# Sums by an adding DMA from GpSimd's queue in place of two GpSimd passes, and a second one-sided part written by ScalarE

## The reference

```python
def attn(x):                      # 16 heads of 16 features, L = 512
    U = min(L, int(5 * math.log(L)))               # 31
    scores = einsum('bhqd,bhkd->bhqk', Q, K) / math.sqrt(16)
    thresh = top_k(scores, U)[0][..., -1:]
    scores = where(scores < thresh, -inf, scores)
    return (softmax(scores) @ V) @ Wo.T + bo

x = x + 0.5 * ffn(layernorm(x))   # 16 gated experts, q/k/v mixed over them
x = x + attn(layernorm(x))
x = x + 0.5 * ffn(layernorm(x))
```

## Time and profile before

| | |
|---|---|
| median of three runs | 4140.59 us (4138.47 to 4140.77) |
| the profiled execution | 4140.48 us, its span 4138.7 us |
| busy, share of the span | PE 94%, DVE 93%, POOL 86%, ACT 85% |
| DMA | 231 MB, mean 56 GB/s |
| granted clock of TensorE | 0.977 over the span |

### The profile page before, as it was taken

The page is one execution under the profiler, slowest core; times in us unless marked ns, Lnnn a source line. Parts: engine busy times, 40 slices in busy tenths (PEclk is TensorE's granted clock), DMA queues, the critical chain, the costliest instruction groups (busy, mean ns, idle before and its releaser), DMA issues.

```text
span 4138.7 us, 97302 instructions
## 1 busy us (share of the span) xinstructions
PE 3891.9 (94%) x31052; PEld 3201.5 (77%) x31052; DVE 3858.8 (93%) x15296; ACT 3530.2 (85%) x7749; POOL 3556.2 (86%) x4554
## 2 busy tenths in 40 slices
PE   6878999999999999999999999999999999998777
PEld 5656788888888888888888888888888888876566
DVE  3399999999999999999999999999999999999982
ACT  3389989989999998999999899999989999998872
POOL 1578999999999999999999999999999999987650
PEclk8889999999999999999999999999999999999988
DMA  3211221212222122222212222222222222121112
GB/s 108 54 34 35 56 63 53 63 56 62 54 58 63 52 63 55 62 55 58 63 52 63 55 60 58 57 61 54 61 56 60 57 58 60 54 50 28 31 29 57
DMA packets 243955, 230.71 MB, mean 56 GB/s; under 512 B 27123, under 2 KB 176628, under 8 KB 243316
## 3 DMA queue, kind: packets, MB, share of 16 engines
q1 hardware_dynamic: 243444, 224.49, 20.7%
HBM read 214.98 MB, written 9.44 MB: 54 GB/s over the span
## 4 chain that ended last, share of the span: by engine, by line
PE 42%; POOL 31%; DVE 18%; ACT 4%; issue 3%; DMA 1%; SPq 0%; POOLq 0%; ACTq 0%; DVEq 0%
PE pQ L592 15%; POOL HS L353 10%; POOL HL L965 5%; POOL HL L964 5%; PE pST L610 4%; PE pST L577 3%; POOL RB L364 3%; PE pFb L553 3%; PE pO L631 3%; DVE HL L915 2%; DVE HL L909 2%; DVE HL L905 2%; DVE HL L901 2%; DVE M L917 2%; DVE M L913 2%
## 5 line engine op out<-in xcount | busy, mean ns | idle before, releaser
L592 PE MATMUL pQ<-wf_sb,HS 128*128 128x192 f32 x8192 | 1474.9, 335 | 87.1 <-POOL HS L353 66.0
L592 PEld LDWEIGHTS pQ<-wf_sb,HS 128*128 128x128 f32 x8192 | 1361.6, 194 | 164.2 <-issue 107.2
L797 ACT ACTIVATE S<-S,edge 128x512 f32<-128x512 f32 x1024 | 743.3, 726 | 7.7 <-POOL edge L952 7.6
L803 ACT ACTIVATE S<-S,lift 128x512 f32<-128x512 f32 x1024 | 747.2, 730 | 1.9
L964 POOL TENSOR_TENSOR HL<-S,HL 128x512 f32<-128x512 f32 x512 | 657.3, 1284 | 12.8 <-ACT S L780 12.8
L965 POOL TENSOR_TENSOR HL<-S,HL 128x512 f32<-128x512 f32 x512 | 657.4, 1284 | 0.0
L610 PE MATMUL pST<-ident,S 128*128 128x128 f32 x4096 | 513.6, 276 | 68.6 <-ACT S L803 41.4
L353 POOL TENSOR_TENSOR HS<-hT_a,RB 128x1024 f32<-128x1024 f32 x244 | 577.8, 2368 | 0.3 <-issue 0.3
L353 POOL TENSOR_TENSOR HS<-hT_b,RB 128x1024 f32<-128x1024 f32 x240 | 568.1, 2367 | 4.1 <-PE pQ L592 2.7
L610 PEld LDWEIGHTS pST<-ident,S 128*128 128x128 f32 x4096 | 460.1, 142 | 107.1 <-ACT S L803 61.1
L780 ACT COPY S<-pST 128x1024 f32<-128x1024 f32 x512 | 494.6, 1025 | 23.1 <-PE pST L577 22.2
(11 more groups left out here) (255 smaller groups left out, 7228.4 us busy)
## 6 DMA issues: line engine op xcount, KB each, us to landing
RB<-rows_b SPq DMA_DIRECT2D x384, 256.0 KB, 3.4
RB<-rows_a SPq DMA_DIRECT2D x384, 256.0 KB, 3.4
x_b<-in_x SPq DMA_DIRECT2D x64, 128.0 KB, 2.1
out_y<-y SPq DMA_DIRECT2D x64, 128.0 KB, 3.1
wf_sb<-in_wf SPq DMA_DIRECT2D x4, 768.0 KB, 7.1
rows_b<-rwT SPq DMA_DIRECT2D x64, 8.0 KB, 1.3
wof_sb<-in_wof SPq DMA_DIRECT2D x1, 1024.0 KB, 7.4
rows_a<-rwT SPq DMA_DIRECT2D x64, 8.0 KB, 1.3
```

What stands on the lines that cost most here:

```text
L592: mm = nc.tensor.matmul(pQ[:, 0:QKV], HS[:, m % 2, e, i, :], wf_sb[:, i, at:at + QKV], start=k + e + i == 0, stop=(k, e, i) == (3, 3, 1))
L797: nc.scalar.activation(S[:, r, :], S[:, r, :], ACT.Prelu, bias=edge[:, r:r + 1], scale=-2.0, alpha=1.0 / STEEP).then_inc(s_cut, 1)
L803: nc.scalar.activation(S[:, r, :], S[:, r, :], ACT.Exp, bias=lift[:, r:r + 1], scale=-0.5 * STEEP).then_inc(s_gap, 1)
```

## The change

The two GpSimd instructions of each pair are gone. For each quad, in slot 4n + 3.5, GpSimd issues one DMA that adds `S` (four units of 512 scores) to what stands in `HL`. For this ScalarE writes both parts in `ED`: the positive part of the difference to the first half of an `HL` entry, and the negative of it to the second half, with a Prelu whose slope is steep on one side and close to zero on the other. The difference is now second minus first (L947), so the first half becomes first + part, the larger, and the second half second - part, the smaller. An `HL` entry has 2 x 272 columns (it had 272 + 256). Each quad's DMA moves 4 x 512 float32 in 128 partitions, 1 MB, in runs of 256 elements (1 KB): 1024 runs. Two semaphores `s_add` take turns; the DMA of quad n waits for all four units of `EV` and for the DMA of quad n - 2. VectorE's `HI8` waits for the whole quad's DMA ahead of the quad's first pair, and for nothing more at `LO8` or at the second pair.

```diff
-AT["SPLIT"] = series(5.75, 2, PAIRS, {0: -2.25, 1: -1.25, 2: 2.75, 3: 4.75, 4: 8.75, 5: 10.75, 6: 12.75, 7: 14.75})
+AT["SPLIT"] = series(3.5, 4, QUADS, {0: -2.9, 1: 2.1, 2: 8.1, 3: 11.1})
...
-        HL = sb("HL", P, RINGH, HIL + HALVES)
+        HL = sb("HL", P, RINGH, 2 * HIL)
...
-                        nc.scalar.activation(HL[:, e:e + 2, HIL:HIL + HALVES], pST[:, h:h + 2, 0:HALVES], ACT.Relu
-                                             ).then_inc(s_rd, 2)
+                        nc.scalar.activation(HL[:, e:e + 2, 0:HALVES], pST[:, h:h + 2, 0:HALVES], ACT.Relu)
+                        nc.scalar.activation(HL[:, e:e + 2, HIL:HIL + HALVES], pST[:, h:h + 2, 0:HALVES], ACT.Prelu,
+                                             scale=-1.0 / STEEP, alpha=STEEP).then_inc(s_rd, 2)
...
-                        if k == HI8:
-                            wait(dve, s_hi, n + 1)
-                        elif k == LO8:
-                            wait(dve, s_lo, n + 1)
-                        else:
+                        if k == HI8 and i == 0 and n % 2 == 0:
+                            wait(dve, s_add[n // 2 % 2], n // 4 * 16 + 16)
+                        elif k not in (HI8, LO8):
...
-                        nc.gpsimd.tensor_tensor(KK[:, c, 1, :], KK[:, c, 0, :], KK[:, c, 2, :], ALU.subtract
+                        nc.gpsimd.tensor_tensor(KK[:, c, 1, :], KK[:, c, 2, :], KK[:, c, 0, :], ALU.subtract
...
-                    r, e = 2 * n % RING, place(2 * n)
-                    first, second = S[:, r:r + 2, 0:HALVES], S[:, r:r + 2, HALVES:T]
-                    hi, lo = HL[:, e:e + 2, 0:HALVES], HL[:, e:e + 2, HIL:HIL + HALVES]
-                    pool.wait_ge(s_ev, 2 * n + 2)
-                    nc.gpsimd.tensor_tensor(hi, second, lo, ALU.add).then_inc(s_hi, 1)
-                    nc.gpsimd.tensor_tensor(lo, first, lo, ALU.subtract).then_inc(s_lo, 1)
+                    r, e = 4 * n % RING, place(4 * n)
+                    pool.wait_ge(s_ev, 4 * n + 4)
+                    wait(pool, s_add[n % 2], n // 2 * 16)
+                    gaps = HL[:, e:e + 4, :].rearrange("p u (a j) -> p u a j", a=2)[:, :, :, 0:HALVES]
+                    nc.gpsimd.dma_start(gaps, S[:, r:r + 4, :].rearrange("p u (a j) -> p u a j", a=2), accum_op=ALU.add
+                                        ).then_inc(s_add[n % 2], 16)
```

More of the change, by code:

```diff
@@ L254, in build @@
         s_kb, s_bop, s_bo, s_half = sem("s_kb"), sem("s_bop"), sem("s_bo"), sem("s_half")
-        s_kd, s_hi, s_lo, s_dif, s_rd, s_edge, s_mid = (
-            sem(n) for n in ("s_kd", "s_hi", "s_lo", "s_dif", "s_rd", "s_edge", "s_mid"))
+        s_kd, s_dif, s_rd, s_edge, s_mid = (
+            sem(n) for n in ("s_kd", "s_dif", "s_rd", "s_edge", "s_mid"))
+        s_add = [sem("s_add0"), sem("s_add1")]
         s_sc, s_ev, s_tk, s_cut, s_lift, s_gap, s_pt, s_pe, s_pv, s_oc, s_ot, s_o, s_vm = (
```

## The result

The changed kernel takes 4371.34 us (median of four, 4368.9 to 4375.43) against 4140.35 us: ratio 1.0558, 95% interval 1.0545 to 1.057. It is slower by 231 us (4371.34 - 4140.35), where 147 were forecast; the time lies in the stated range and in the likeliest case's own (4195 to 4510). The profiled execution took 4375.43 us, its span 4373.6.

The account below looks back on a forecast made before the run. TensorE, VectorE and GpSimd were taken as within some 2% of the period, GpSimd's delays showing on TensorE. -3.6 + 5.9 + 6.9 = +9.2 us a sequence, 16 times +147, gave 4288 us; range 4130 to 5000 us.

Parts of the forecast that it names:

- the likeliest case: The forecast itself, issue between 1 and 4 us: 4195 to 4510 us, chance 0.44.
- Relief: GpSimd loses two instructions a pair; all TensorE waits for "hs" credited: -3.6 us a sequence.
- The second instruction: ScalarE's added instruction a pair lengthens ED by 0.98 us a quad, delaying SC: +5.9 us a sequence.
- The six tight quads: Quads of a sequence where TensorE already waits to start SC; each loses 0.98 us, +5.9 us a sequence.
- as load it fits: ScalarE's added 15.7 us a sequence fits into its 21.9 us of spare time.
- The issue: GpSimd's DMA issue behind EV, taken as 2.4 us, delays "hs" and TensorE's products: +6.9 us a sequence.
- chain against room: From SC to products: chain of 4.7 to 5.6 us plus issue, its excess over each quad's room summed.
- The transfer: Adding DMA from S to HL takes 7.9 us, late for most quads at VectorE's search, but priced 0.
- The bound by the issue's load: Rival: GpSimd becomes the bound by its issue; 4705 us at 5 us, 5840 at 9.5; chance 0.20.
- The late landing: Rival: the add lands late and VectorE waits, or DMA engines are full: 4900 us; chance 0.09.
- The faster kernel: Rival: issue under 1 us and TensorE later into tight quads: 4083 us, or 4130; chance 0.12.
- the bound of one microsecond: Sign on GpSimd: the prediction is wrong if "hs" follows EV within a microsecond.

Follow-up runs that it names:

- the ladder: The first four experiments: from a kernel with only GpSimd's relief left, one part of the change comes back at a time; beside a kernel before of 4139.7 us.
- run 2: As run 1, with both ScalarE instructions a pair, the second another Copy to the entry's other half: 4233.19 us.
- run 11: As run 2, with the second ScalarE instruction reading SBUF, behind both first parts: 4196.22 us.
- run 1: Changed kernel without adding DMA and wait for EV, one ScalarE instruction a pair writing a constant that VectorE searches: 4097.31 us.
- run 3: As run 2, with GpSimd waiting for the quad's EV in slot 4n + 3.5 but issuing nothing: 4236.6 us.
- run 5: As run 3, with an ordinary GpSimd addition of 700 columns behind the wait, in place of the DMA: 4287.49 us.
- Run 9: Complete changed kernel with each issue later in GpSimd's order, behind hs and LIFT: 4258.41 us.
- run 4: As run 3, with the adding DMA issued, its sums unread: VectorE searches constants in a tile of its own: 4374.62 us.
- run 6: As run 4, with 32 elements instead of 256 in each of the DMA's 1024 runs: 4373.26 us.

## Why the forecast was right, and where it was off

The 231 us are made up, by the ladder, of -42 (relief), +136 (second ScalarE instruction), +3 (wait for EV), +138 (issue), -3 (landing, no difference). The forecast's terms were -58, +94, 0 within the chain, +110 and 0. The time fell in the stated range because that range allowed for an issue of 1 to 4 us; the sum itself was 84 us short.

- **Relief: right.** 42 us were had of 58 credited, within the bound of 64.
- **The second instruction: right in sign, too small, and its reason wrong in two steps.** The first is the count of the delayed quads. The forecast let the second half of `SC` follow the first by 0.53 us, so that in ten quads of a sequence "0.98 us hardly shows". But the four heads run side by side, and in four of the ten the late fourth instruction parts them (run 2: 1.14 to 1.70 us). The six tight quads cost 5.3 us a sequence where 5.9 were forecast; with the other four it is 7.5 us, 120 in all. The second step is "as load it fits". When run 11 takes SC's delay away, 99 us over run 1 remain, 43 of TensorE's at `TR` and 25 at the transposes of `Sr`. So ScalarE's 21.9 idle us a sequence weren't all spare: the added work makes other results late that TensorE waits for. What part of run 2's 136 us is of this kind isn't shown, since there SC has 125 of them.
- **The issue: right mechanism, two errors that partly cancelled.** The estimate of 2.4 us was too high: 1.63 us by its row, 1.83 with the later start. The Trainium skill's rule (DMA: Bandwidth & Descriptors, "Anatomy of one DMA — SWDGE (gpsimd) path"), that many descriptors come before the extra cost shows, holds in part: 512 runs more cost 0.27 us in the row. That was worth 47 us here. What was mis-sized is the room. The forecast's own rule of chain against room gives 3.8 us a sequence for 1.83 us, 61 us in all; 138 were measured. That the total of 110 came as near as it did is luck: too long an issue stood in for a chain left out. It had named LIFT and CUT as queued behind the wait and priced hs alone. The trace of run 3 tells what room was left before an issue came. Summed over the quads, 1.83 us is longer than the room between the end of hs and TensorE's products by 74 us, and longer than that between LIFT and CUT by 137 us (quads 30 to 225, scaled to 256); for the 1.29 us of run 5 it is 24 and 69 us, and 51 were measured. By this count hs alone falls short of what was measured. Run 9, which puts the issue behind both, takes 113 us back. It doesn't part the two, and on TensorE the loss shows at the products: from run 3 to run 4 its idle time before them rises from 34.0 to 126.7 us and their busy time by 31.5. That a late CUT reaches them through a later EV and hs is argued, not shown. That the wait itself is free and only the issue costs came out as forecast.
- **The transfer: right.** VectorE waits for it at 131 of the 256 quads, 154.7 us in all, but this costs nothing (run 4). By the page the adding queue holds the DMA engines for 0.443 x 4373.6 / 256 = 7.6 us a quad; 7.9 were estimated, twice a plain copy. The Trainium skill (Collectives: The Full Stack, "The bandwidth ceiling") has half the rate for a ReduceScatter, whose add takes two source reads; the 7.6 us agree with such a factor.
- **The rivals.** The bound by the issue's load didn't come: GpSimd is at 62%. The late landing didn't come before the issue was moved. The faster kernel would have needed both parts of the change to be free.
- **The signs.** The four instructions of `ED` take 2.06 us, as said. SC is drawn out in 10 quads of a sequence, not in 6. "hs" starts 1.3 us after EV, close to the bound of one microsecond that would have called the forecast wrong; that distance understates the issue, since "hs" starts before the issue has ended and is drawn out.

Open: a plain delay of exactly 1.83 us wasn't tried, so that a DMA issue hurts no more than an equal addition rests on the order of four points, not on a pair. The two chains behind the issue weren't delayed one by one either.

## What to carry to other kernels

Before an operation moves to a place right behind a late wait, list what stands behind it in that engine's queue and measure for each the room to its consumer; load saved on the engine says nothing about it. One slot later in the order was worth 113 of 138 us here. And idle time of an engine that waits for the bound inside a two-way exchange isn't room for work in front of what the bound waits for: 0.98 us a quad on an engine at 91% cost 136 us, and 99 us still when it was out of the way of its first consumer. Before you call a delay hidden because only half of a group waits for it, look whether the halves run one after the other or side by side.

## What the runs showed of the hardware

- A DMA issued by GpSimd from SBUF to SBUF with an add costs the engine 1.63 us for 1024 runs and 1.36 us for 512, whatever their length (1024 runs of 32 or 256 elements: 1631 ns both; 512 runs of 256 or 512: 1368 and 1362 ns). From these two counts that is, as an estimate, some 1.1 us and 0.5 ns a run. It starts 0.30 us after the end of the instruction waited for; "hs" or `LIFT` in its place (run 3) starts after 0.08.
- The next GpSimd instruction starts 1.0 us into the issue and ends as late as if it had waited: 2.98 us for 2.37, and 0.85 for 0.21 where it is the small first step of `LIFT` (median of 71 quads). Its row hides part of the issue's cost.
- An adding DMA of 1 MB lands after 9.6 us, one of 128 KB in the same number of runs after 4.3. Plain loads of 256 KB beside the large one land in 4.7 to 6.4 us instead of 3.4, which cost nothing here (runs 4 and 6, 4374.6 and 4373.3 us).
- TensorE's products for four heads with 32 rows each start within 0.02 us of each other and take 1.14 us together. Where two of the four must wait, the quad takes two passes: 1.70 us with a wait that ended 0.52 us after the start of the first two.
